# Operators of three folded cross attentions: the values' formed and stored first, and in the last attention the products between the groups of its norm

## What is computed

```python
H = 16; DH = 64
xn = layer_norm(x, g_x, b_x)
cn = layer_norm(context, g_c, b_c)
q = (xn @ Wq).reshape(B, N, H, DH).transpose(0, 2, 1, 3)
k = (cn @ Wk).reshape(B, M, H, DH).transpose(0, 2, 1, 3)
v = (cn @ Wv).reshape(B, M, H, DH).transpose(0, 2, 1, 3)
sim = jnp.einsum('bhid,bhjd->bhij', q, k) * DH ** -0.5
attn = jax.nn.softmax(sim, axis=-1)
out = jnp.einsum('bhij,bhjd->bhid', attn, v)
out = out.transpose(0, 2, 1, 3).reshape(B, N, INNER)
return out @ Wo
```

## The kernel before

| products | x0c | x2c | x3c | shape | evicted by |
|---|---|---|---|---|---|
| keys `kt` (two matmuls each) | 8 | 2 | 8 | 128x154 | ACT even n, DVE odd n |
| values `vt` (two matmuls each) | 8 | 2 | 8 | 128x154 | ACT even n, DVE odd n |
| keys' operator (lines 2335, 2379, 2413) | 16 | 8 | 32 | 128x154 | each by ACT (upper f16 part), then DVE (the rest) |
| values' operator (lines 2345, 2379, 2413) | 16 | 8 | 32 | 77x256 | each by ACT (upper f16 part), then DVE (the rest) |

## Time and profile before

### The profile page before, as it was taken

The page is one execution under the profiler, slowest core; times in us unless marked ns, Lnnn a source line. Parts: engine busy times, 40 slices in busy tenths (PEclk is TensorE's granted clock), DMA queues, the critical chain, the costliest instruction groups (busy, mean ns, idle before and its releaser), DMA issues. The chain is left out here.

```text
span 3315.8 us, 43986 instructions
## 1 busy us (share of the span) xinstructions
PE 2489.6 (75%) x15362; PEld 1385.1 (42%) x15362; DVE 1861.2 (56%) x5005; ACT 1432.4 (43%) x2891; POOL 978.9 (30%) x802
## 2 busy tenths in 40 slices
PE   6978886597544668888875669886776788957977
PEld 2323334465332333333353255555443233345666
DVE  4476664465657655555522548324442577655678
ACT  4324442364331146666621414213511355636876
POOL 1045562135455456666621310000201101101200
PEclk9979998798777889999987879998788799968988
DMA  3211100530264421111001210111000322014023
GB/s 110 73 41 41 45 19 30 164 111 27 87 195 79 96 70 34 42 45 40 22 14 51 48 40 1 42 70 33 14 0 26 79 28 35 9 47 121 2 77 102
DMA packets 185740, 182.86 MB, mean 55 GB/s; under 512 B 55161, under 2 KB 152187, under 8 KB 184751
## 3 DMA queue, kind: packets, MB, share of 16 engines
q1 hardware_dynamic: 176110, 167.48, 18.1%
q0 software_dynamic: 9408, 12.56, 2.5%
HBM read 121.81 MB, written 61.59 MB: 55 GB/s over the span
## 5 line engine op out<-in xcount | busy, mean ns | idle before, releaser
L929 POOL TENSOR_TENSOR l1a_p_lo<-res,l1a_p_hi 128x1024 f16<-128x1024 f32 x192 | 311.7, 1642 | 174.1 <-ACT res L1170 174.1
L1179 ACT ACTIVATE l0a_probs<-ps 128x1024 f32<-128x1024 f32 (+1 forms) x192 | 145.6, 810 | 175.2 <-PE ps L1033 103.1
L1179 ACT ACTIVATE l3a_probs<-ps 128x1024 f32<-128x1024 f32 (+1 forms) x192 | 146.6, 808 | 140.5 <-PE ps L1033 113.4
L1169 ACT ACTIVATE l1a_p_hi<-ps 128x1024 f16<-128x1024 f32 x192 | 157.9, 823 | 112.2 <-PE ps L1033 81.6
L1030 PE MATMUL ps<-l1a_qs,l1a_ks 128*128 128x512 f16 (+3 forms) x768 | 165.4, 329 | 32.7 <-ACT res L1170 32.7
L1201 DVE CUSTOM_DVE_ANT_0 l1a_masked<-ps,l1a_wide_mask 128x128 bf16<-128x128 f32 (+3 forms) x256 | 118.0, 489 | 103.0 <-PE ps L999 100.6
L954 POOL TENSOR_TENSOR l0a_both<-l0a_probs 128x768 f32<-128x768 f32 (+2 forms) x96 | 154.5, 1631 | 46.4 <-PE ps L1071 46.1
L999 PE MATMUL ps<-l1a_ks,l1a_qs 128*128 128x512 f16 (+3 forms) x384 | 120.5, 342 | 63.3 <-DVE l1a_nmax L1204 33.1
L2752 PE MATMUL ps<-x_m,x_x 128*128 128x462 f16 (+1 forms) x672 | 135.8, 350 | 31.2 <-PEq L111 30.5
L1170 ACT ACTIVATE res<-ps 128x1024 f32<-128x1024 f32 x192 | 158.5, 826 | 0.0
L1033 PE MATMUL ps<-mask_t,ident_b 128*128 128x128 bf16 x768 | 156.4, 224 | 0.0
(11 more groups left out here) (732 smaller groups left out, 6307.4 us busy)
## 6 DMA issues: line engine op xcount, KB each, us to landing
f_wf<-in_L_ffn_w_dram SPq DMA_DIRECT2D x16, 1024.0 KB
f_slots<-x0a_zeros SPq DMA_DIRECT2D x32, 256.0 KB
f_xe<-f_slots SPq DMA_DIRECT2D x32, 256.0 KB, 3.0
f_ys<-f_y SPq DMA_DIRECT2D x32, 256.0 KB
l1a_qs<-l_q_h SPq DMA_DIRECT2D x64, 128.0 KB
d_wall<-in_L_ffn_W_dram SPq DMA_DIRECT2D x3, 2112.0 KB
l0a_qs<-l_q_h SPq DMA_DIRECT2D x32, 128.0 KB
l0a_ks<-l_k_h SPq DMA_DIRECT2D x16, 256.0 KB
```

The source lines that it names most:

```text
L929: pool.tensor_tensor(ph_lo[:, n % SLOTS, :, 0:w], probs[:, n % FULL, :, 0:w], ph_hi[:, n % SLOTS, :, 0:w], ALU.subtract).then_inc(s_["low_ ...
L1169: act.activation(ph_hi[:, n % SLOTS, :, 0:w], SB[n % 2][:, :, 0:w], ACT.Exp)
L1179: act.activation(probs[0:KR, n % SLOTS, 2 * pr:2 * pr + 2, 0:w], SB[x % 2][:, :, 0:w], ACT.Exp).then_inc(s_["exps"], 1)
```

## The change

`cross_operators` is written anew around functions that issue a span of products, and two things in the program's order change.

1. In all three attentions the values' operator comes ahead of the keys' operator (n_m and the end of the values' operator swap their places in the count), SP waits for the evictions of the values' operator only ahead of the stores, and Wq is loaded last instead of ahead of Wv and Wo. PE now waits ahead of the values' operator, not ahead of the keys', for the evictions of kt and vt.
2. In x3c `norm_program` takes an object `within` that each engine calls in each group g: for g = 1 it does the norm of the context, for g = 2 the eight products kt, for g = 3 the eight products vt.

```diff
@@ norm_program, vector
             normed(g)
+            if within:
+                within.vector(dve, g)
             if parts and g >= 2:
                 lower(g - 2)
@@ norm_program, scalar
             if g >= 1:
                 columns(g - 1)
+            if within:
+                within.scalar(act, g)
         columns(NG - 1)
@@ norm_program, tensor
             ins.then_inc(ph.s["n_turned"], 1)
+            if within:
+                within.tensor(pe, g)
@@ cross_operators
         n_k, n_v = FC, 2 * FC
-        n_m = n_v + DC * H
-        NJ = n_m + B * H
+        n_m = n_v + B * H
+        NJ = n_m + DC * H
+        SHARES = (0, 0, n_k, n_v)
...
+            def products(pe, n0, n1):
+                for n in range(n0, n1):
+                    if n == n_k:
+                        pe.wait_ge(ph.s["v_ld"], 32)
+                    if n == n_v:
+                        pe.wait_ge(ph.s["o_ld"], 16)
+                        pe.wait_ge(ph.s["by_act"], acts(n_v))
+                        pe.wait_ge(ph.s["by_dve"], lowers(n_v))
+                    if n == n_m:
+                        pe.wait_ge(ph.s["q_ld"], 16)
+                    free(pe, n)
...
+                def inner_vector(dve, g):
+                    if g == 1:
+                        context_rows(dve)
+                    if g > 1:
+                        lower_evictions(dve, SHARES[g - 1], SHARES[g])
...
+                norm_program(ph, block, None, *columns, [k.ps[:, 6:8, :]], parts=parts, within=within)
+            done = n_v if columns is not None else 0
...
                 for dst, src in first:
                     sp.dma_start(dst, src).then_inc(ph.s["k_ld"], 16)
-                sp.dma_start(wq[:], weight_rows(wqt)).then_inc(ph.s["q_ld"], 16)
                 for dst, src in second:
                     sp.dma_start(dst, src).then_inc(ph.s["v_ld"], 16)
                 sp.dma_start(wos[:], weight_rows(wo)).then_inc(ph.s["o_ld"], 16)
-                sp.wait_ge(ph.s["by_act"], acts(NJ))
-                sp.wait_ge(ph.s["by_dve"], lowers(NJ))
+                sp.dma_start(wq[:], weight_rows(wqt)).then_inc(ph.s["q_ld"], 16)
+                sp.wait_ge(ph.s["by_act"], acts(n_m))
+                sp.wait_ge(ph.s["by_dve"], lowers(n_m))
```

More of the change, by code:

```diff
@@ L220, in tensor, with norm_program @@
         ins.then_inc(ph.s["xn_turned"], 1)
-def norm_program(ph, block, x_in, xnt, w_col, b_col, TP, parts=None):
+def norm_program(ph, block, x_in, xnt, w_col, b_col, TP, parts=None, within=None):
     k = ph.k
@@ L2261, in cross_operators @@
         ph.sems_of("k_ld v_ld q_ld o_ld cleared chain sd_ready turned cols prods by_act by_dve vp_st x_upper x_lower")
+        within = Within() if columns is not None else None
         bank = [k.ps[:, i, :] for i in range(4)]
         n_k, n_v = FC, 2 * FC
-        n_m = n_v + DC * H
-        NJ = n_m + B * H
+        n_m = n_v + B * H
+        NJ = n_m + DC * H
+        SHARES = (0, 0, n_k, n_v)
         def acts(n):
@@ L2360, in place, with turned_context @@
                 return v_st[part][:, h * B + b if shared else b * H + h, :], bank[n % 4][0:M, 0:D], 1.0
-            @block.scalar
-            def _(act):
-                if columns is None:
-                    for g in range(NG):
-                        act.activation(parts[0][:, :, g * GN:(g + 1) * GN], k.xtr[:, :, g * GN:(g + 1) * GN], ACT.Copy).then_inc(ph.s["x_upper"], 1)
+            def turned_context(pe):
+                pe.wait_ge(ph.s["cleared"], 3)
+                pe.wait_ge(ph.s["k_ld"], 16 * len(first))
+                if norm is not None:
+                    pe.wait_ge(ph.s["chain"], 2 * B + 3)
+                    for b in range(B):
+                        pe.transpose(k.ps[:, 4, b * P:b * P + M], rows[:, b, 0:P], k.ident[0:M, 0:M])
+                        ins = pe.transpose(k.ps[0:CR, 5, b * P:b * P + M], rows[:, b, P:CTX], k.ident[0:M, 0:M])
+                    ins.then_inc(ph.s["turned"], 1)
+                    pe.wait_ge(ph.s["cols"], 2 * B)
@@ L2373, in _, with evictions @@
                         act.activation(cb[0:CR, b * M:(b + 1) * M], k.ps[0:CR, 5, b * P:b * P + M], ACT.Identity, scale=nb[:, 0:1], bias=nb[:, 1:2]).then_inc(ph.s["cols"], 1)
-                for n in range(NJ):
+            def evictions(act, n0, n1):
+                for n in range(n0, n1):
                     if n < n_v and n % 2:
@@ L2398, in _, with lower_evictions @@
                     ins.then_inc(ph.s["chain"], 1)
[L2399 to L2404 removed]
+            def lower_evictions(dve, n0, n1):
+                for n in range(max(n0, 1), n1):
                     if n < n_v and n % 2 == 0:
@@ new lines, in _ @@
+            @block.tensor
+            def _(pe):
+                if columns is None:
+                    turned_context(pe)
+                products(pe, done, NJ)
+            @block.scalar
+            def _(act):
+                if columns is None:
+                    for g in range(NG):
+                        act.activation(parts[0][:, :, g * GN:(g + 1) * GN], k.xtr[:, :, g * GN:(g + 1) * GN], ACT.Copy).then_inc(ph.s["x_upper"], 1)
+                    context_columns(act)
+                evictions(act, done, NJ)
@@ L2415, in _ @@
+            @block.vector
+            def _(dve):
+                if columns is None:
+                    context_rows(dve)
+                    for g in range(NG):
+                        t = slice(g * GN, (g + 1) * GN)
+                        dve.wait_ge(ph.s["x_upper"], g + 1)
+                        dve.tensor_tensor(parts[1][:, :, t], k.xtr[:, :, t], parts[0][:, :, t], ALU.subtract).then_inc(ph.s["x_lower"], 1)
+                lower_evictions(dve, done, NJ)
                 dve.wait_ge(ph.s["x_lower" if columns is None else "n_lower"], NG)
```

127 lines of the change are left out of this document (60 added, 67 removed).

## The result

| | before | after |
|---|---|---|
| median of 5 runs, us | 3321.72 | 3299.38 |
| lowest and highest | 3313.7, 3328.15 | 3294.99, 3306.51 |
| the profiled execution, its span | 3317.57, 3315.8 | 3301.9, 3300.1 |
| mean granted TensorE clock | 0.887 | 0.880 |

The ratio of after to before is 0.9936, 95% interval 0.9918 to 0.9955: about 21 us faster.

What follows compares the result with a forecast made beforehand. No engine bounds the whole; the touched phases end with stores while no engine works. Gains 4.8 + 2.6 + 10.9 = 18.3 us, from 3317.57 to 3299.3, plus 4.15 for a median: 3303.4, range 3296 to 3311.

Steps and rivals of the forecast that it cites:

- In all three the stores stay the later end: x0c, x2c, x3c: stores of 7.25, 4.3 and 12.9 us outlast keys' operators of at most 5.6, 2.8 and 11.0.
- x0c and x2c: Values' operator ends at 627.2 instead of 631.97 and 2304.5 instead of 2307.08; gains 4.8 and 2.6 us.
- PE's new wait for the last vt: x0c: PE must wait for the last vt's eviction ahead of the values' operator; costs about 0.9 us.
- The interleaving gives nothing: x3c: first operator eviction at 2979.5, before 2979.39; some 14 us hidden come back as waits in one chain.
- 13.5 us more: x3c: values' operator from first eviction at 2979.5 to 2993.0 instead of 3003.92, a gain of 10.9 us.
- The transfer's length: x3c's stores: the trace's 12.9 us taken instead of 7.8 by the Trainium skill's formula.
- The forecast's 8.4 us for that case: x3c's gain if stores took 7.8 us, less than the keys' operator; 8.4 instead of 10.9, sum 15.8.
- Late Wk: Rival, x3c: Wk lands at the bound of 2960.9, costing 9.6 us; sum 8.7, time 3313; chance 0.05.
- stores that do not run ahead: Rival: SP's stores gain nothing by the early start, so 4.8 + 2.6 + 10.9 are gone; 3321.7; chance 0.03.
- Half clock: Rival, x3c: all 16 products run at 1.2 GHz, 6.6 us more; sum 11.7, time 3310; chance 0.15.
- Slower by the clock of the rest: Rival: PE's mean clock elsewhere falls to 0.870, 29 us net, 3351; decides from 0.880 on; chance 0.03.
- Wrong altogether if the phases outside differ by more than a few us in sum: Sign that would refute the prediction: phases outside x0c, x2c and x3c differing by more than a few us in sum.

Runs made afterwards that it cites:

- store_late: The changed kernel, but SP waits for the evictions of both operators ahead of the stores; ratio to before 1.0027.
- swap_only: The changed kernel with only values' operator first, stored early, and Wq loaded last; no interleaving in x3c; ratio to before 0.9944.
- after again: The changed kernel run once more without edit; 3305.56 us, ratio to before 0.9960.
- split: The changed kernel with each store cut in two, the first half issued when half the values' operator is evicted; ratio to before 0.9917.
- both: The changed kernel with x3c's evictions reordered behind the norms and each store cut in two; 3287.16 us, ratio to before 0.9901.
- reorder: The changed kernel with x3c's kt evictions behind the last norm and root, DVE's subtractions spread between evictions; ratio to before 0.9927.
- between_only: The changed kernel with only x3c's interleaving; keys' operator first, old load order, one store at the end; ratio to before 1.0009.
- before again: The kernel before run once more without edit; 3317.93 us, ratio to before 0.9992.

## Why the prediction was right, point by point

**The measure.** 3303.4 was forecast, 3299.38 measured, inside 3296 to 3311. The three phases' gain is 17.4 us against 18.3, and `store_late` and `swap_only` show that it comes from the cause named. The whole is a coarser witness: 15.7 us between the two profiled executions, 21 by the first ratio, 13 by that of after again.

**"In all three the stores stay the later end": right.** The gaps without an engine were forecast at about 3, 2.5 and 3.5 us ahead of x0a, x2a and x3a, and are 636.74 - 633.77 = 3.0, 2.7 and 3005.91 - 3003.39 = 2.5 (DVE's last eviction of x3c ends at 3003.39), all ended by SP's wait. The bounds 5.6 and 2.8 us for the keys' operator held in x0c and x2c (5.44 and 2.85). In x3c it was said to take at most 11.0, and took 12.5: that bound was read from the earlier trace rows as if the clock came with the instructions, and the clock fell in it (0.53 from 2996.0 on). It did not show in the time because the store still ended later, by 1.7 us: the gap of 2.5 less the 0.8 that `split` and `both` show behind a last eviction. With a store shorter by more than that the operator would have set the end.

**x0c and x2c: right.** In x0c the forecast 627.2 for the last value is 27.0 us after the phase's start, and it came at 628.41, 26.6 after. PE's new wait for the last vt is there, as a first eviction 1.41 us behind the last copy where 1.2 was said. In x2c 2.2 instead of 2.6 us: the store took 1.41 + 3.1 = 4.5 us where 4.3 were taken, and the first value and the operator were 0.2 and 0.1 us later.

**"The interleaving gives nothing": right.** `swap_only` has 65.6 without it, after 65.8 with it. The waits named are in the rows of after: the context's norm ahead of the third group's as PE's 3.18 us, the last group's root and L265 behind the evictions of kt as its 3.05 us, and the subtractions as its 2.43 us. But two terms were off and cancelled, which is luck. The first value's eviction was forecast for 37.6 us and came at 35.8: the context's norm followed the last L265 without any wait for Wk (0.55 had been charged), and the transposes, the vt and the subtractions were each some tenths quicker. The step that failed the other way is "13.5 us more": that block took 15.0. The clock was 0.50 from 35.8 to 42.7 us after the phase's start, and it fell while PE stood idle for 2.43 us; in `swap_only` and `reorder`, at 1.00, the same block took 13.2. By an estimate from these rows, 65.7 - 1.8 = 63.9 against `swap_only`'s 65.6, the interleaving would have been worth 1.7 us at full clock. I had asked for the clock in the products, which were fast, and had not carried it to the operator behind the subtractions. Together the values' operator ended 11.3 us earlier than before instead of 10.9. The store then took 13.9 instead of 12.9: 11.3 - 1.0 = 10.3, and 10.2 was measured.

**The transfer's length.** The trace's 12.9 us was taken over the 7.8 that follow from the Trainium skill, "DMA: Bandwidth & Descriptors", section "Anatomy of one DMA". The runs decide for the trace: 12.8 to 13.9 in every whole store of x3c. By 7.8 the keys' operator would have set the end, and `split` could have gained nothing there; it gained 2.0. (The forecast's 8.4 us for that case takes the keys' operator at about 10.3 us, which no row of it shows; with its own bound of 11.0 it would be 7.7.)

**The rivals.** Late Wk and stores that do not run ahead are excluded by the rows of after. Half clock is excluded in its own place: the kt ran in 5.3 us, as forecast, not 8.6. A fall behind idle PE appeared one step later, and in `between_only` with a larger price. The Trainium skill states in "TensorE: Matmul & The Clock Gate", section "What's actually happening", that the default state is throttled and that activity releases the throttle. The falls behind idle PE agree with it (0.50 behind 2.43 us); the fall in a busy keys' operator is not explained by it. Slower by the clock of the rest: the mean clock did fall, from 0.887 to 0.880, just where I had said that it decides, and the program was 21 us faster. The 0.887 was no property of the kernel before: 33 further executions of it lie at 0.873 to 0.884, with a median of 0.880, and the 12 of after again have the same median. The rival was priced from one high execution.

**"Wrong altogether if the phases outside differ by more than a few us in sum": kept, but it says little.** Outside the three phases the span is 3315.8 - 137.0 = 3178.8 us before and 3300.1 - 119.6 = 3180.5 after, 1.7 us apart. That is luck, for single phases moved by up to 15 us up and down, and between two executions of one kernel the same sum moved by 4.4 us (before) and 6.7 us (after). The stretch x2a with the feed forward behind it, in the profile of before, in before again, and in after:

```profile
2312.43:2536.30 223.87, 163.92 (x724) 99.91 (x724) 92.58 (x288) 74.37 (x248) 20.93 (x23) 0.86 0.03 9
```

```profile
2299.96:2540.00 240.04, 180.81 (x724) 108.38 (x724) 93.09 (x288) 74.73 (x248) 20.95 (x23) 0.77 0.03 8
```

```profile
2293.69:2532.69 239.00, 179.91 (x724) 107.89 (x724) 92.97 (x288) 74.67 (x248) 20.93 (x23) 0.78 0.03 8
```

The same 724 matmuls took 163.92 us of PE at a clock of 0.86 and 180.81 at 0.77. The stretch is 16.2 us longer in the second execution of the unchanged kernel, and in after again 229.6. So the 15 us that after "lost" here are no effect of the change. Of the 9.4 it "won" between x0a and the next layer's first load (316.4 to 307.0), 7.0 are gone in before again (309.4); the other 2.4 are no more than what this stretch varies by among the kernels with the new order (306.6 to 309.3). The rival drew on a true thing with a wrong cause: the clock of the rest moves without the change. The runs of before spread over 14 us; how much of that is the clock is not shown.

## What to carry to other kernels

Where a phase ends with a transfer and nothing runs beside it, form what it stores first and let the wait ahead of it cover only that; the gain is how much earlier it starts, as long as the transfer stays the later end. Putting products into gaps of a norm paid here only when nothing of theirs stood ahead of the norm's own steps in any queue: against no interleaving the same products gave 0 us with the evictions ahead of the last norm and three subtractions behind them, and 8 us with the evictions behind the norm and the subtractions spread. The two moves were not run apart. Judge such an edit by the phases it touches, in more than one execution of both kernels and with the clock read in each, before believing a difference of the whole.

## What was not expected of the hardware

- The granted clock fell to the lower level (1.2 GHz) in the middle of busy work, in x3c's keys' operator, whose products have 64 rows. Counted from its first eviction on DVE, it fell after 5.6 us in after, 5.7 in after again, 5.5 in `swap_only`, 5.8 in `store_late` (with no transfer), 6.2 in `split`, 3.0 in `reorder` and 9.8 in `both`. In before, where the keys' operator comes first, it did not fall: PE was busy for 9.57 of 10.51 us at 1.00, and 5.67 of 5.80 us ahead of the fall in after again. The two rows are before, and `both` up to shortly behind its fall:

```profile
2979.39:2989.90 10.51, 9.57 (x61) 7.85 (x62) 8.45 (x32) 7.85 (x31) 0.00 (x0) 1.00 0.00 0
...
2968.30:2978.50 10.20, 9.86 (x59) 7.84 (x58) 8.36 (x30) 8.17 (x30) 0.00 (x0) 0.98 0.44 127
```

What decides it was not found.

- A short idle stretch can cost more than itself. Behind 3.10 us of idle PE in `between_only` 13.1 us of matmuls ran at 0.52. Behind 2.43 us in after the clock was 0.50 for 6.4 us, and the values' operator took 1.8 us more than in `swap_only`. Behind the 3.05 us ahead of after's last transposes it was 0.50 for 3.3 us, in which the first two vt took 1.03 us each, against 0.52 for the last:

```profile
2965.80:2969.10 3.30, 3.30 (x16) 3.30 (x14) 0.00 (x1) 0.30 (x1) 0.00 (x0) 0.50 0.00 0
```

- A store of 2.5 MB from 77 partitions took 12.8 us from its first issue to SP's release in the four executions in which PE, DVE and ACT were idle beside it (before, before again, `between_only`, `store_late`). Beside the keys' operator it took 12.8 in `swap_only`, 13.3 in `reorder`, 13.6 in after again and 13.9 in after.
